# A relational graph layer with layernorm on one core: the last pair transposed as packed bytes, one batch fewer loaded by units, and a pair's transposition moved between two products

## The reference

```python
rel_ids = jnp.arange(1, weight.shape[0] + 1, dtype=relation.dtype)
masks = (relation[None] == rel_ids[:, None, None, None]).astype(x.dtype)
h = jnp.einsum('rbnm,bmd->rbnd', masks, x)
y = jnp.einsum('rbnd,rdo->bno', h, weight)
x = _layernorm(x + y + bias, axis=-1)
```

## Time and profile before

| | us |
|---|---|
| median of 3 runs | 113.28 (113.25 to 113.73) |
| the profiled execution | 113.02 |
| its span | 110.9 |
| PE busy | 101.1 |
| ACT busy | 84.8 |
| DVE busy | 81.9 |
| POOL busy | 76.8 |

### The profile page before, as it was taken

How to read it: one execution, slowest core, us unless ns; L and a number is a source line. 1 busy time by engine, 2 the same in 40 slices (tenths; PEclk the granted TensorE clock), 3 DMA queues, 4 the chain that set the end, 5 groups by cost and what they waited for, 6 DMA issues and landing times.

```text
span 110.9 us, 2869 instructions
## 1 busy us (share of the span) xinstructions
PE 101.1 (91%) x1017; PEld 89.4 (81%) x1017; DVE 81.9 (74%) x246; ACT 84.8 (77%) x104; POOL 76.8 (69%) x139
## 2 busy tenths in 40 slices
PE   5869999989995999999999999999999999999900
PEld 2249889989995999989988998899889988999900
DVE  1033667479775999689968996899689968997970
ACT  3074969988399896999699969986999699956750
POOL 3000800780399899989998999899989997906860
PEclk9999999999999999999999999999999999999997
DMA  3999999999999999999999999999999999996054
GB/s 72 370 418 403 414 406 409 406 408 420 423 408 426 420 423 405 420 414 414 417 417 414 423 420 414 412 418 420 414 411 426 420 414 411 409 420 281 1 214 177
DMA packets 8369, 42.21 MB, mean 381 GB/s; under 512 B 929, under 2 KB 1058, under 8 KB 5282
## 3 DMA queue, kind: packets, MB, share of 16 engines
q1 hardware_dynamic: 8208, 41.49, 92.0%
q10 hardware_dynamic: 146, 0.52, 1.4%
HBM read 37.81 MB, written 4.19 MB: 379 GB/s over the span
## 4 chain that ended last, share of the span: by engine, by line
PE 72%; DVE 8%; DMA 5%; issue 4%; POOL 4%; ACT 4%; POOLq 0%; ACTq 0%
PE h_ps L632 44%; PE ids_t L610 12%; PE y_ps L645 10%; PE ids_t L601 6%; DMA adj_sb<-adj 5%; DVE mask_t L743 4%; ACT bytes_of L500 3%; POOL x_sb L467 2%; DVE row_max L733 1%; DVE stats L756 1%; DVE moments L767 1%; DVE x_sb L806 1%; ACT x_sb L532 0%; POOL product L450 0%; POOL product L444 0%
## 5 line engine op out<-in xcount | busy, mean ns | idle before, releaser
L500 ACT ACTIVATE bytes_of<-adj_sb,offset 128x2048 fp8e4<-128x2048 int32 x32 | 64.1, 2004 | 5.1 <-DMA adj_sb<-adj 4.7
L743 DVE TENSOR_SCALAR mask_t<-ids_t 128x1024 uint16<-128x1024 uint16 x63 | 40.9, 682 | 15.4 <-PE ids_t L601 12.3
L632 PE MATMUL h_ps<-mask_t,x_hi 128*128 128x256 bf16 (+1 forms) x272 | 34.0, 269 | 0.9 <-DVE mask_t L743 0.9
L632 PE MATMUL h_ps<-mask_t,x_lo 128*128 128x256 bf16 (+1 forms) x272 | 34.0, 269 | 0.0
L632 PEld LDWEIGHTS h_ps<-mask_t,x_hi 128*128 128x128 f16 x272 | 24.7, 100 | 3.9 <-DVE mask_t L743 1.8
L632 PEld LDWEIGHTS h_ps<-mask_t,x_lo 128*128 128x128 f16 x272 | 25.7, 100 | 2.6
L428 POOL TENSOR_TENSOR x_sb<-x_sb,bias_sb 128x1024 f32<-128x1024 f32 x8 | 19.0, 2379 | 10.3 <-ACT bias_sb L551 9.8
L467 POOL TENSOR_SCALAR x_sb<-x_sb,rstd,shift 128x128 f32<-128x128 f32 x55 | 23.9, 453 | 1.7 <-DVE shift L801 0.8
L422 POOL TENSOR_TENSOR x_lo<-x_sb,x_hi 128x1024 f16<-128x1024 f32 x7 | 15.0, 2145 | 6.6 <-ACT x_hi L513 6.1
L610 PE MATMUL ids_t<-ident,bytes_of 128*128 128x128 bf16 x184 | 15.8, 229 | 1.5 <-ACT bytes_of L500 1.2
L610 PEld LDWEIGHTS ids_t<-ident,bytes_of 128*128 128x128 bf16 x184 | 13.9, 149 | 3.9 <-ACT bytes_of L500 3.8
(11 more groups left out here) (54 smaller groups left out, 42.7 us busy)
## 6 DMA issues: line engine op xcount, KB each, us to landing
adj_sb<-adj SPq DMA_DIRECT2D x24, 1024.0 KB, 24.6
adj_sb<-adj SPq DMA_DIRECT2D x16, 512.0 KB, 11.0
x_sb<-x SPq DMA_DIRECT2D x7, 512.0 KB, 24.0
out<-x_sb SPq DMA_DIRECT2D x7, 512.0 KB, 19.8
x_sb<-x ACTq DMA_DIRECT2D x1, 512.0 KB, 5.1
out<-x_sb SPq DMA_DIRECT2D x2, 256.0 KB, 2.2
w_sb<-weight SPq DMA_DIRECT2D x1, 64.0 KB, 7.9
bias_row<-bias ACTq DMA_DIRECT2D x1, 0.5 KB
```

Source lines behind the costliest of these rows:

```text
L500: nc.scalar.activation(bytes_of[:, at % ROOM].rearrange("p n t -> p t n"), adj_sb[:, slot, 2 * k:2 * k + 2, :], ACT.Square, scale=SLOPE, b ...
L632: last = nc.tensor.matmul(h_ps[g.bank][:, to], part[:, g.b % 2, j, :], mask_t[:, g.b % 2, j, cols], start=(j == 0 and part is x_hi), stop= ...
L743: nc.vector.tensor_scalar(mask_t[:, b % 2, :, u * P:(u + 1) * P].bitcast(UINT16), ids_t[bank_of(turn)][:, :, :].bitcast(UINT16), 1 << bit, ...
```

## The change

It has three parts. EARLY goes from 2 to 1, so that batch 1 is loaded in four transfers of a pair instead of eight of a unit. The last pair is packed like the others: one transposition after its check takes the place of two, and the mask of d is made by DVE behind that of e instead of by ACT; with it the order of some steps in the tail changes on ACT and DVE. And in the steady part, when a group works on its first pair, the hi products come ahead of the transposition of its second pair, and the lo products behind it.

```diff
-    EARLY = 2
+    EARLY = 1
...
     def packed(b, k):
-        return FIRST_PACKED <= pair_no(b, k) < PAIRS * B - 1
+        return pair_no(b, k) >= FIRST_PACKED
...
             load_x(1)
-            for u in range(J):
-                load_unit(1, u)
-            load_x(2)
             for b in range(EARLY, B):
                 for k in range(PAIRS):
                     load_adj(b, k)
-                if b + 1 < B:
-                    load_x(b + 1)
+                    if k == PAIRS - 1 and b + 1 < B:
+                        load_x(b + 1)
...
             copy_h(a)
             root(full)
-            mask_last(d)
             normalise(full, full.units[4:5])
...
             normalise(full, full.units[7:]).then_inc(s_aside, 1)
-            normalise(ra, ra.units[2:3])
             root(rb)
-            normalise(ra, ra.units[3:]).then_inc(s_aside, 1)
+            normalise(ra, ra.units[2:]).then_inc(s_aside, 1)
...
             def step_by_two(g, units, b, k):
-                if packed(b, k):
+                if packed(b, k) and units[0] == g.first:
+
+                    products(g, units, x_hi)
+                    transpose_pair(b, k)
+                    products(g, units, x_lo)
+                elif packed(b, k):
                     transpose_pair(b, k)
...
             a, c, e, d = groups[LAST:]
-            transpose_unit(e.b, e.first)
+            transpose_pair(e.b, e.first // 2)
             products(c, c.units, x_hi)
-            transpose_unit(d.b, d.first)
             project(a)
...
             mask_unit(e.b, e.first)
+            mask_unit(d.b, d.first)
             offer_guess(r)
...
             statistics(e)
+            combine(rb, e, e.units)
             statistics_of_sum(d)
-            combine(rb, d, range(J - 2, J))
+            combine(rb, d, d.units)
```

More of the change, by code:

```diff
@@ L219, in adj_resnorm_kernel @@
         s_mask = sem("units_masked")
-        s_mask_last = sem("last_unit_masked")
         s_check = sem("pairs_checked")
@@ L534, in normalise @@
                 return last
[L536 to L541, removed]
             act.dma_start(units_of(x_sb[:, 0], 0, 0, J), rows_of(x, 0, 0, J)).then_inc(s_x[0], 16)
@@ L615, in products @@
                 if part is x_hi:
[L616 to L619, removed]
+                    pe.wait_ge(s_mask, unit_no(g.b, units[-1]) + 1)
                     if g.index:
```

## The result

The changed kernel is slower. Its five executions took 114.08 to 116.69 us, median 115.57, beside 113.41 for the kernel before in the same session; the ratio is 1.0123, 95% interval 1.009 to 1.0155, or +1.4 us. The forecast was 114.9, range 114.0 to 115.5: by the ratio the first result is 113.28 + 1.4 = 114.7, inside the range, while the median of all five stands 0.07 above it.

What follows compares the result with a forecast made beforehand. It took the loads to set the pace, with PE nearly as tight (0.47 us slack a batch), and PE and DVE after the change. +0.70 + 0.61 + 0.61 - 0.29 = +1.63 on 113.28 gave 114.9 us, range 114.0 to 115.5.

Steps and rivals of the forecast that it cites:

- Loads of batch 1: Loading batch 1 by pairs: same bytes and order, taken as 0, with ends of -0.2 and +0.1 us.
- Term 1: Steady loop: PE waits 0.55 us for DVE's masks in each batch's first group, delaying batch 7's first hi products: +0.70.
- rival A: Loads stay the pace in the loop, so the mask waits add 0; sum +0.93, 114.2 us; chance 16%.
- Term 2: Batch 7: pair 29's transposition ends later behind the hi products, and all of it reaches DVE's guess: +0.61 us.
- term 3: Tail: the mask of d moves to DVE ahead of the guess for batch 6, delaying it: +0.61 us.
- What the guess holds: Tail: the late guess moves POOL's shift, ACT's copy of c and PE's project(c) by 1.92 us; PE waits 1.4.
- Rival B: Tail: the guess holds nobody and PE's own way is the longer; +0.2, 113.5 us; chance 6%.
- Term 4: From project(c) to the last row: root(rb) comes earlier (-0.20), moments of e are taken before d (-0.09); -0.29 us.
- POOL's way to 108.85: Tail: POOL's shift, blocks and roots of ra end at 108.85, in time before rb's shift at 109.3.
- C: Loop: DVE's masks are in time, needing at most 3.85 us instead of 4.40; faster, 112.2 us; chance 5%.
- D: Tail: the clock falls in PE's 1.4 us wait before project(c), doubling 2 us of PE work; 116.9 us; chance 3%.
- E: Loop: the two orders of hi products and transposition come to the same, as DVE sets both; 113.3 us; chance 4%.

Runs made afterwards that it cites:

- order_alone: Kernel before with only the hi products put ahead of the transposition of a group's second pair; 113.88 us, ratio 1.0061.
- guess_first: Changed kernel with DVE's guess for batch 6 put ahead of the mask of d; 113.79 us, ratio 1.0037 against the kernel before.
- the repeat: Changed kernel run once more, unchanged, with six executions; 114.29 us beside 113.26 for the kernel before, ratio 1.0079.
- copies_first: Changed kernel with ACT's copies of c and e put ahead of its first normalised block of batch 6; 113.88 us, ratio 1.0057 against the kernel before.
- tail_mended: Kernel before with batch 1 loaded by pairs, last pair packed, guess ahead of mask of d, copies of c and e first, PE's old order; 112.65 us, ratio 0.9935.
- before_late: Kernel before with 12 idle matmuls (2.56 us) on PE ahead of group 1; 113.37 us, ratio 1.0005.
- loads_alone: Kernel before with only batch 1 loaded by pairs; 113.0 us, ratio 0.9976.
- after_late: Changed kernel with 12 idle matmuls (2.56 us) on PE ahead of group 1; 117.04 us, ratio 1.0256 against the kernel before.

## Why the prediction was right or wrong

The direction and the chain came as forecast. The agreement of the number is in part luck: two terms were off and two things were missing, and without late executions the kernel costs +0.9, not +1.63. The first session's +1.4 stands nearer to the forecast, but it rests on three executions, 114.08, 114.54 and 115.57, and what made the last of them late, the cause of the traced one or another, isn't in the prediction.

- **Loads of batch 1**: I took 0; in the kernel before it is -0.28. The rows had it (2% on 10 us), and I set it aside because PE and DVE would be the pace. In the kernel before they are not; that it arrives in the changed kernel too is argued from the sum of the parts (+0.87 beside +0.9), which has an uncertainty as large.
- **Term 1, the mask waits: +0.70 forecast, +0.24 measured** (T of batch 7 minus T of batch 2 is 56.08, before 92.70 - 36.86 = 55.84). The place is right, a wait of PE on DVE's masks in each of batches 2 to 6. The size isn't: I took 1.21 from the row maxima to the sum, and in the loop of the changed kernel it is 1.12 (42.05 to 43.17), so that the wait was 0.46 instead of 0.55. A term that counts five batches multiplies an error of 0.1 by five. That comes near rival A's number. Its mechanism isn't that of the changed kernel, whose PE waits for no check after pair 8 and takes 11.21 to 11.22 us a batch in each of its traces; but it is that of order_alone, where with the loads by units the pace stays theirs, 11.25.
- **Term 2, pair 29 later, and term 3, the mask of d**: +1.22 forecast, guess at T + 8.94 for 8.96. order_alone (guess +0.70 with T +0.09) shows the one alone, guess_first (-0.59) the other.
- **What the guess holds**: project(c) at T + 11.50 forecast at 11.53, PE's wait 1.34 forecast at 1.4. Rival B (the guess holds nobody) fell; the transposition and the ACT work saved brought nothing, as written.
- **Term 4: -0.29 forecast, -0.14 measured** (the last row 5.06 after project(c), before 5.20). The root starts 0.03 behind the last moments, as forecast, but the two moments are now taken apart, e's between the statistics of e and d, and d's statistics start 2.68 after project(c) instead of 2.55. (POOL's way to 108.85 in this part adds up to 108.56 as it is written; the rest are gaps between its steps, and nothing hangs on it.)
- **Sum by the measured sizes**: 0.24 + 1.19 - 0.14 = +1.29, and with the loads +1.01, for +0.9 (+1.03 between the medians) measured in the repeat.
- **Missing: the late start.** I read PE's slack of 0.47 a batch as something that lets PE follow the loads, and priced its loss by the mean pace alone. That it also absorbs whatever delays PE early I didn't ask. It made +2.1 in the profiled execution and, if the other late executions are of the same kind, moved the median of the first session from about 114.3 to 115.57.
- **Rivals**: C (the masks in time) fell by the same waits; D (the clock falls in the wait) fell, behind the wait of 1.34 the sets of small products stand 0.45 apart (107.39 and 107.84), as they did ahead of it (104.44 and 104.89); E fell, as the two orders differ by 0.69 (order_alone).

## What to carry to other kernels

Ask of a change in a steady loop not only what it does to the mean pace, but whether the loop can still run faster than its feed: slack on the second-tightest engine is what takes back a late start, and its loss costs little in an execution that starts in time (+0.69 here) and all of the delay in one that doesn't (+2.0 to +2.3 for 2.56). In a queue worked through in order, look what stands ahead of a cheap step whose input has long been there; here a copy of 0.4 us and a reciprocal of 0.2 us carried the end, and moving them turned the packed last pair from a loss (+0.46) into part of a gain (-0.7 with the loads). And when one such wait is removed, read the next engine's timeline for gaps first: with a DVE without any, the last row came earlier by half of what PE gained, 0.75 of 1.5 in copies_first and 0.31 of 0.65 in tail_mended.

## What the runs showed of the hardware

TensorE's fast pace began at different times in the same program: 16 transpositions at 14 us took 1.91 us in one execution of the changed kernel and 1.16 in another. The clock row of the page tells part of it. In before_late (1.84 us) and loads_alone (1.86 us) the same eight transpositions that take 0.7 us at the fast pace take it early, at 6.3 and 6.7 us, then need 1.06 to 1.08 from some 8.5 to 15.7 us, and the row falls to between 5 and 7 just there (from 11.2 to 14.0 us the granted clock is 0.50 in both, the lower of the two levels, 1.2 GHz). In the late execution of the changed kernel eight transpositions need 1.05 to 1.07 from the first on up to 16.4 us, and the row reads 9 all the while. So in the first 16 us a low row meant the slow pace, but a row of 9 didn't mean the fast one; the durations of identical matmul groups do tell. A late fast pace isn't the change's doing, as before_late has it with the loads by units; whether the kind under a row of 9 is, can't be said: up to 16 us it is in two traces, that of the changed kernel and that of after_late.
